# Layer 1 of a two-layer graph network: x1 loaded and base stored in four transfers of 640-byte packets instead of one of 2560

## The reference, cut to what matters

```
x = _layernorm(x + _L0_gnn_ref(x, node_vec1, src, dst, edge_attr_4, edge_attr_64, ...), axis=-1)
x = _layernorm(x + _L1_gnn_ref(x, node_vec1, edge_attr_16, edge_attr_4, src, dst, ...), axis=-1)
```

```
sc = jnp.concatenate([x0 @ Wsc0 * a * inv8, (jnp.einsum('num,uv->nvm', x1, Wsc1) * a[..., None] * inv32).reshape(n, 3 * MUL1)], axis=1)
...
return sc + alpha * conv
```

## Time and profile before

| | |
|---|---|
| median of 3 runs | 2080.49 us (2071.84 to 2082.07) |
| profiled execution, its own time | 2057.88 us |
| its span, first to last instruction | 2055.1 us |
| PE, DVE, ACT, POOL busy | 1436.3, 1438.8, 1062.9, 1474.8 us |
| layer 0 edge stage | about 50 to 740 us |
| layer 0 node stage | about 740 to 1080 us |
| layer 1 edge stage | about 1084 to 1796 us |
| layer 1 node stage | about 1796 to 2055 us |
| DMA packets and bytes | 253883, 439.92 MB |
| queue q1 (SyncE's transfers) | 152304 packets, 311.47 MB |
| queue q0 (GpSimd's transfers) | 75264 packets, 67.79 MB |

### The profile page before, as it was taken

One profiled execution on the slowest core, in us unless ns is written; L12 is line 12 of the kernel. 1 busy time (PEld: TensorE's weight loads), 2 busy tenths in 40 slices (PEclk: granted clock), 3 DMA queues, 4 the chain that ended last, 5 costly groups with the idle time before them and its releaser, 6 DMA issues.

```text
span 2055.1 us, 48034 instructions
## 1 busy us (share of the span) xinstructions
PE 1436.3 (70%) x10424; PEld 1275.1 (62%) x10424; DVE 1438.8 (70%) x5759; ACT 1062.9 (52%) x3600; POOL 1474.8 (72%) x1923
## 2 busy tenths in 40 slices
PE   5078888788888848888876998999989999300000
PEld 4067777677777737676755888888888888300000
DVE  5067777677777719999983665666656666289998
ACT  3034444444444418999973554554545454146676
POOL 3067888777787647888873777777777777468887
PEclk9589999999999979999997999999999999755555
DMA  9967666676666749999954777777777777499997
GB/s 385 430 151 134 133 137 136 135 132 136 136 135 134 178 101 340 339 337 338 340 208 138 166 167 166 167 170 167 164 162 170 161 169 162 80 362 402 400 399 294
DMA packets 253883, 439.92 MB, mean 214 GB/s; under 512 B 33424, under 2 KB 131152, under 8 KB 250576
## 3 DMA queue, kind: packets, MB, share of 16 engines
q1 hardware_dynamic: 152304, 311.47, 45.1%
q0 software_dynamic: 75264, 67.79, 24.3%
q10 hardware_dynamic: 26208, 59.65, 7.5%
HBM read 235.50 MB, written 203.27 MB: 214 GB/s over the span
## 4 chain that ended last, share of the span: by engine, by line
PE 26%; issue 21%; POOL 13%; ACT 13%; DVE 9%; DMA 6%; SPq 4%; another core or an unknown queue 3%; ACTq 3%; DVEq 1%; POOLq 0%
ACT y L845 9%; POOL table L500 7%; POOL xg L483 5%; DVE stats L1081 3%; SPq L374 3%; DMA table<-sums,row_all 3%; PE ps L679 3%; DVE res L1042 3%; PE ps L660 2%; PE ps L641 2%; PE ps L627 2%; PE ps L643 2%; ACTq L857 2%; PE ps L669 2%
## 5 line engine op out<-in xcount | busy, mean ns | idle before, releaser
L500 POOL DMA_INDIRECT table<-sums,row_all x392 | 630.9, 1609 | 316.4 <-issue 131.2
L782 ACT COPY msg<-ps 128x192 f32<-128x192 f32 (+1 forms) x196 | 57.4, 293 | 680.9 <-PE ps L660 495.8
L845 ACT ACTIVATE y<-res,norm 128x160 f32<-128x160 f32 x756 | 330.3, 507 | 125.8 <-POOL norm L536 69.0
L991 DVE SCALAR_TENSOR_TENSOR x1g<-ps,a_all,x1g 128x160 f32<-128x160 f32 x392 | 132.3, 379 | 200.2 <-PE ps L680 95.3
L483 POOL DMA_INDIRECT xg<-in_x_rows,src_all x196 | 201.8, 1029 | 59.6 <-issue 58.7
L483 POOL DMA_INDIRECT xg<-x_rows,src_all x196 | 195.8, 999 | 64.3 <-issue 58.5
L641 PE MATMUL ps<-weights,midT 128*128 128x128 f32 (+1 forms) x784 | 164.0, 293 | 86.9 <-DVE msg L951 84.8
L946 DVE TENSOR_TENSOR pe<-ps,ea_all 128x192 f32<-128x192 f32 x196 | 69.8, 356 | 185.1 <-ACT msg L782 99.8
L1081 DVE BATCH_NORM_STATS2 stats<-res 128x6 f32<-128x160 f32 x784 | 196.0, 311 | 3.8 <-issue 0.3
L641 PEld LDWEIGHTS ps<-weights,midT 128*128 128x128 f32 x784 | 127.2, 204 | 94.9 <-issue 87.7
L534 POOL TENSOR_TENSOR half_rstd<-var,minus_half 128x8 f32<-128x8 f32 x98 | 165.0, 1683 | 14.2
(11 more groups left out here) (115 smaller groups left out, 4465.4 us busy)
## 6 DMA issues: line engine op xcount, KB each, us to landing
tab<-table SPq DMA_DIRECT2D x98, 384.0 KB, 5.0
table<-zeros SPq DMA_DIRECT2D x24, 1536.0 KB
table<-zeros SPq DMA_DIRECT2D x98, 324.0 KB
tab<-table SPq DMA_DIRECT2D x98, 324.0 KB, 5.4
xzT<-in_xzT SPq DMA_DIRECT2D x98, 320.0 KB, 4.9
x1g<-x_rows SPq DMA_DIRECT2D x98, 320.0 KB
base_rows<-x1g SPq DMA_DIRECT2D x98, 320.0 KB
x1g<-base_rows SPq DMA_DIRECT2D x98, 320.0 KB, 4.9
```

The costliest lines, as they stand in the source:

```text
L500: pool.indirect_dma_start(out=table[l], out_offset=bass.IndirectOffsetOnAxis(ap=row_all[:, at:at + 1], axis=0), in_=sums[j % 4][:, t, 0:W] ...
L845: last = nc.scalar.activation(y[u][:, t, :], res[u][:, t, :], ACT.Identity, scale=rstd[u][:, t:t + 1], bias=shift[u][:, t:t + 1])
L991: last = stt(x1g[v][:, 2 * b + t, :], n1_ps[:, t, :], a, x1g[v][:, 2 * b + t, :], ALU.mult, ALU.add)
```

## The change

`load_x1` and `store_base` each issue four transfers, one for each tile t, in place of one. Each has 128 packets of 640 bytes. In HBM the rows of one tile lie 2560 bytes apart. Every piece counts 16 on the same semaphore as before, so the waits of SyncE, TensorE (`turn1`) and ScalarE (`copy_z1`) now ask for 64 counts per group. Nothing else is changed.

```
 def load_x1(g, m, u):
     v = u % 4
-    wait_count(sp, s_bstore[v], landed(g - 4, first_of(v, 4), 4))
+    wait_count(sp, s_bstore[v], landed(g - 4, first_of(v, 4), 4, 16 * T))
     sp.sem_inc(s_sptick, 1)
-    sp.dma_start(x1g[v][:, :, :].rearrange("p t c -> p (t c)"),
-                 x1_rows[bass.ds(m * GROUP, GROUP), :].rearrange("(p t) c -> p (t c)", t=T)).then_inc(s_x1[v], 32)
+    rows = x1_rows[bass.ds(m * GROUP, GROUP), :].rearrange("(p t) c -> p t c", t=T)
+    for t in range(T):
+        sp.dma_start(x1g[v][:, t, :], rows[:, t, :]).then_inc(s_x1[v], 16)
...
 def store_base(g, m, u):
     v = u % 4
     sp.wait_ge(s_z1, 2 * (g + 1 - NG))
-    sp.dma_start(base_rows[bass.ds(m * GROUP, GROUP), :].rearrange("(p t) c -> p (t c)", t=T),
-                 x1g[v][:, :, :].rearrange("p t c -> p (t c)")).then_inc(s_bstore[v], 16)
+    rows = base_rows[bass.ds(m * GROUP, GROUP), :].rearrange("(p t) c -> p t c", t=T)
+    for t in range(T):
+        sp.dma_start(rows[:, t, :], x1g[v][:, t, :]).then_inc(s_bstore[v], 16)
...
# turn1 (TensorE), copy_z1 (ScalarE)
-    pe.wait_ge(s_x1[v], landed(g, first_of(v, 4), 4, 32))
+    pe.wait_ge(s_x1[v], landed(g, first_of(v, 4), 4, 16 * T))
```

More of the change, by code:

```diff
@@ L450, in _ @@
                     for u in range(4):
-                        sp.wait_ge(s_bstore[u], landed(2 * NG - 4 + (u - 2 * NG) % 4, first_of(u, 4), 4))
+                        sp.wait_ge(s_bstore[u], landed(2 * NG - 4 + (u - 2 * NG) % 4, first_of(u, 4), 4, 16 * T))
                     run_stages(sp, NG, NG, 10, [(0, load_base), (2, load_table)], RING)
@@ L801, in copy_z1 @@
                     v = u % 4
-                    act.wait_ge(s_x1[v], landed(g, first_of(v, 4), 4, 32))
+                    act.wait_ge(s_x1[v], landed(g, first_of(v, 4), 4, 16 * T))
                     wait_count(act, s_nT, 2 * (g - 1 - NG))
```

## The result

The changed kernel takes 2135.05 us (median of 4 runs, 2133.97 to 2136.96) against 2076.16 us of before (4 runs). The ratio is 1.0289, interval 1.0244 to 1.0335: slower, as forecast, but by 59 us and not by 265. The time lies 60 us under the lower end of my range. Ratios are formed from undisturbed executions where these could be told apart, and so can differ in the third digit from the quotient of the medians.

What follows compares the result with a forecast made beforehand. TensorE, with GpSimd close, bounded before; SyncE's queue would bound the change. Its turn: 6.10 + 4.32 - 0.5 - 0.2 = 9.72 us; 88 turns cost 256 us, with ends 264, giving 2345 us, range 2195 to 2435.

Steps and rivals of the forecast that it cites:

- the serial string of store, landing and load: SyncE's queue, layer 1 edge stage: each load waits for the store just ahead; turn forecast to reach 9.72 us.
- TensorE's clock: Rival: TensorE falls to 1.2 GHz, turn at most 12.6 us, 2598 us; lower clock or more, chance 0.06.
- the small packets: Term (4), DMA engines: 864 more packets a turn at 5.7 ns, 0.31 us a turn, hidden.
- the last store piece to the first load: SyncE's queue: time from last store piece to first load forecast at about 3.1 us.
- the loss of slack: SyncE's wait for VectorE's x1g, 0.71 us a turn before, forecast to be nearly gone.
- the falling DMA share: Layer 1 edge stage: DMA share forecast to fall below 0.75, same bytes spread over more time.
- TensorE's share: Layer 1 edge stage: TensorE forecast to be busy near 65% of the stage.
- (1): SyncE's queue: six added issues a turn at a gap of 0.72 us each, 4.32 us a turn.
- the 6.10 us of work on the queue: SyncE's occupied time per turn before the change: 6.81 us turn less 0.71 us slack.
- my rival of cheap issues: SyncE's added issues: gap only 0.43 to 0.60 us, 2191 us, or 2281 at 0.60; chance 0.15.
- 6.81 us as before's turn: Layer 1 edge loop: one turn before the change, read from 88 base stores, set by TensorE, GpSimd just under.
- my low end: SyncE's queue: cheap issues at gap 0.43 us, turn 7.98 us, 2191 us; the range began at 2195 us.

Runs made afterwards that it cites:

- four_large: Before with load and store of x1 and base each split by partitions into four issues of 32, packets of 2560 bytes: 2135.3 us, ratio 1.0195.
- pause8: Before with 8 semaphore increments on SyncE's queue behind each load of x1: 2034.9 us, ratio 0.9837; repeated in another job, 2089.7 us, ratio 1.0234.
- pause16: Before with 16 semaphore increments on SyncE's queue behind each load of x1: 2044.0 us, ratio 0.9889.
- One_small_lag3: Before with one issue each way in 640-byte packets and store_base one turn earlier (lag 3 for 4): 2088.4 us, ratio 1.0183.
- before_again: The kernel of before, no edit, run and profiled again in the first job: 2090.4 us.
- split_load: Before with only the load in four pieces of 640-byte packets, the store as one transfer: 2129.4 us, ratio 1.0376.
- lag3: The changed kernel with store_base one turn earlier (lag 3 for 4): 2080.9 us, ratio 0.9947 against before.
- two_large: Before with load and store each split into two pieces of 64 partitions, packets of 2560 bytes: 2098.5 us, ratio 1.0247.
- one_small: Before with one issue each way but packets of 640 bytes: 2035.6 us, ratio 0.9732; repeated in another job, 2072.8 us, ratio 1.0107.
- before_third: The kernel of before, no edit, run and traced in the fourth job: 2067.9 us.

## Why the prediction was wrong

**What held.** SyncE's queue became the bound; the serial string of store, landing and load is its cause; TensorE's clock was no matter (0.95 in the stage, with the engine busy 83% of it); the small packets were hidden, at 5.5 ns each where I had 5.7; the last store piece to the first load took 2.96 us where I had 3.1; the count of packets, the loss of slack, the falling DMA share (0.70 for 0.75) and the new entries of the chain came as written. TensorE's share came out at that 83% and not at the 65% I wrote, because the turn grew less.

**The term that was mis-sized** is (1), the gap of 0.72 us, and with it the 6.10 us of work on the queue to which it was added. Measured: 0.49 to 0.54 us for each gap, in every kernel with four pieces, with stalls elsewhere or without. That is 3.1 us for 4.32, or 106 us of the kernel's time at 88 turns, half of the 206 us by which the forecast's loss was too high. The rest of the string is 4.75 us where I had 5.40: the last store piece to its landing 2.74, and the four other gaps 0.22, 0.61, 0.60 and 0.58. That is another 57 us, nearly all of it stalls that I had left in the three gaps behind the load. Sum 7.87 for 9.72 us. The measured gap lies in the 0.43 to 0.60 of my rival of cheap issues, to which I gave 0.15. It had 7.98 us for s = 0.43, nearer in sum than in its parts, and it too gave too long a time.

**Why it too gave too long a time** is a second step that failed: the side the string was compared with. I took 6.81 us as before's turn and TensorE's work as its bound. In the traces without stalls, like that of after, before's turn is 7.20 and 7.25 us, and its floor is GpSimd's 6.4. 7.87 - 7.22 = 0.65 us x 88 = 57 us, against a measured 59 us in the result (no trace tells whether before's four runs there had stalls) and 45 us for four_large; the 0.41 us between 6.81 and 7.22 are 36 us of the miss. With stalls it is 8.0 - 6.81 = 1.19 us x 88 = 105, against 117. So the change's price differs with the state of SyncE's queue: with stalls the change is longer and before shorter. Each state was seen on chips of its own, so what differs between chips otherwise isn't told apart from it.

**Where I could have seen it.** The rows showed the issue itself at 0.36 us and also as short as 0.01, with the stall outside it, against steady ones in the head and in the last stage. I explained that by GpSimd's issuing, but GpSimd is as busy in after's layer 0, where the stalls are gone (412.15 us of 130 to 640 us, against 408.65 in before). And my low end assumed that the stalls stay in the base while they go from the pieces; with both gone, 0.43 us for a piece and 0.67 for each of the three other gaps, the string would have been 6.10 + 2.58 - 0.5 - 0.45 = 7.73 us and the time some 2170 us, still too high for the second reason.

**What stays open.** Why the queue stalls in some executions, whether by chip or by launch. All traces of one job agree, but before's first trace and after's don't, and I don't know whether those two shared a chip; the five jobs ran on five chips, so the two causes can't be told apart. And by what path the transfers delay gathers and scatters: that the timing of the queue moves before's turn from 7.2 to 6.5 us is shown by pause8, and to 6.8 by pause16; that it is the collision on the DMA engines is only argued, from the waits that shrank. One_small_lag3 speaks a little against it: at 7.15 us a turn GpSimd waits almost never for its scatters to land.

```profile
POOL table L502 <- DMA table<-sums,row_all: 0.8, 1, 0.8
```

## What to carry to other kernels

On a queue that issues a transfer, waits for it to land and issues the next, sum up the whole turn with the landing in it, and compare it with the turn of the engines, before adding an issue: here each added issue cost 0.5 to 0.7 us as soon as the sum passed theirs. The size of the packets did not matter; a smaller last piece shortened the landing, by 0.2 us against before_again and by 1.6 us against split_load. Let a load wait for a store that was issued a turn earlier: that took the whole loss away with all eight issues in place (lag3). And check that the time of an instruction is the same in a part of the program that no one has changed, in more than one trace, before building a sum on it.

## What the runs showed of the hardware that I hadn't expected

- SyncE's queue has stalls in some executions and not in others, for the same code. From one issue to the next in layer 0's loop: 0.88 and 0.91 us on average in the trace of before, 0.62 and 0.57 in before_again. A semaphore increment took 0.06 us without them and 0.11 to 0.15 with them. Runs of four like DMAs with only register work between them kept 0.49 to 0.54 us in both.
- An issue didn't hold SyncE's queue equally long in all shapes: 0.33 to 0.36 us for 128 partitions and for 32, 0.53 us for the 64-partition pieces of two_large, 0.62 us for the store of 512 packets in one_small. So two_large's pairs are 0.69 and 0.58 us apart, more than the gaps in a run of four. No run tells why.
- Adding 0.5 us of waiting per turn on a queue that had slack made the kernel 1.6% faster (pause8, interval 0.8 to 2.4%), where the same edit on another chip made it 2.3% slower.
- The landing of a 320 KB store issued at once took 2.8 to 4.2 us by kernel: 2.81 in before_third, 3.73 in pause8, 3.95 in split_load, 4.18 with small packets. It doesn't go with the speed: pause8 was faster than its before and split_load slower.
- A packet of 640 bytes instead of 2560 in queue q1 was worth nothing either way while the queue was the bound (2129.4 against 2123.4 us); an added packet took 5.5 ns of one DMA engine (the change against four_large).
